# Slot starts of a mixture-of-experts layer: a running sum by doubling, replaced by a product with a triangle and one row sum

## The reference

```python
xn = _layernorm(x)
x = x + attention(xn, Wq, Wk, Wv, Wo) + moe(xn, gate_w, expert_w, expert_b)
# attention: 16 heads of 32, rotary positions, causal softmax
# moe, for each token:
gate_logits = xf @ gate_w.T                      # 8 experts
top_vals, top_idx = top_k(gate_logits, 2)
w = softmax(top_vals)                            # the two shares
y_all = einsum('td,eod->teo', xf, expert_w) + expert_b
out = sum(take_along_axis(y_all, top_idx) * w)
```

## Time and profile before

| what | value |
|---|---|
| median of 3 runs | 982.35 us (981.11 to 984.5) |
| the profiled execution's own time | 979.72 us |
| its span, first to last instruction | 977.9 us |
| PE busy | 915.0 us (94%) |
| DVE busy | 739.1 us (76%) |
| POOL busy | 559.2 us (57%) |
| ACT busy | 436.7 us (45%) |
| DMA queue of SP, share of 16 engines | 44.9% |
| mean granted TensorE clock | 0.992 |

### The profile page before, as it was taken

One profiled execution on the slowest core, in us unless ns is written; L12 is line 12 of the kernel. 1 busy time (PEld: TensorE's weight loads), 2 busy tenths in 40 slices (PEclk: granted clock), 3 DMA queues, 4 the chain that ended last, 5 costly groups with the idle time before them and its releaser, 6 DMA issues.

```text
span 977.9 us, 18755 instructions
## 1 busy us (share of the span) xinstructions
PE 915.0 (94%) x6589; PEld 450.1 (46%) x6589; DVE 739.1 (76%) x1327; ACT 436.7 (45%) x711; POOL 559.2 (57%) x553
## 2 busy tenths in 40 slices
PE   2899898989999989989999999998999999999887
PEld 1344344444444544545555555544444444444333
DVE  7988988898889899944444444467788888888865
ACT  5367877766765443421122211134344444344432
POOL 1545686674776446753333333148877888777741
PEclk9999999999999999999999999999999999999999
DMA  6365688688786362586655555455655564555431
GB/s 245 108 227 186 193 272 320 197 309 299 222 287 245 120 217 88 201 285 191 197 175 176 177 174 173 151 195 163 205 179 182 170 196 141 164 184 184 151 110 55
DMA packets 107963, 188.63 MB, mean 193 GB/s; under 512 B 11872, under 2 KB 65248, under 8 KB 102624
## 3 DMA queue, kind: packets, MB, share of 16 engines
q1 hardware_dynamic: 97072, 152.03, 44.9%
q0 software_dynamic: 10800, 35.40, 12.9%
HBM read 117.13 MB, written 70.25 MB: 192 GB/s over the span
## 4 chain that ended last, share of the span: by engine, by line
PE 69%; DVE 14%; ACT 6%; DMA 4%; issue 3%; POOL 3%; SPq 1%; DVEq 0%; ACTq 0%; POOLq 0%
PE psum L945 19%; PE psum L1030 11%; PE psum L1054 7%; PE psum L993 6%; PE psum L980 5%; PE psum L996 5%; PE psum L962 5%; PE psum L1039 4%; DVE top L1479 4%; PE psum L922 3%; ACT pT L760 2%; PE psum L964 2%; DMA sum_sb<-x 2%; ACT x_in L693 1%; DMA w_rows<-w_hl 1%
## 5 line engine op out<-in xcount | busy, mean ns | idle before, releaser
L760 ACT ACTIVATE pT<-psum,factors 128x512 f32<-128x512 f32 (+1 forms) x352 | 217.9, 642 | 239.9 <-PE psum L980 231.3
L1479 DVE TENSOR_REDUCE top<-psum 128x1 f32<-128x384 f32 (+3 forms) x352 | 209.9, 635 | 19.9 <-PE psum L964 18.9
L1030 PE MATMUL psum<-xT,w_att 128*128 128x512 f16 x768 | 196.6, 382 | 7.7 <-DVE xT L1430 5.1
L945 PE MATMUL psum<-w_exp,x_gT 128*128 x852 | 195.3, 379 | 0.8 <-DVE x_gT L1435 0.8
L610 POOL DMA_INDIRECT x_g<-xn_rows,tok_of x71 | 67.3, 948 | 131.8 <-PE psum L922 129.1
L962 PE MATMUL psum<-k_stack,q_stack 96*128 96x384 f16 (+3 forms) x512 | 127.4, 302 | 13.8 <-DVE top L1479 13.1
L980 PE MATMUL psum<-q_stack,k_stack 98*128 98x256 f16 (+3 forms) x512 | 128.6, 303 | 11.6 <-ACT pT L760 9.1
L1435 DVE TENSOR_TENSOR x_gT<-psum,x_gT 128x512 f16<-128x512 f32 x71 | 49.0, 691 | 104.1 <-ACT x_gT L784 86.8
L945 PEld LDWEIGHTS psum<-w_exp,x_gT 128*128 128x128 f16 x852 | 83.4, 98 | 85.8 <-issue 1.1
L784 ACT ACTIVATE x_gT<-psum 128x512 f16<-128x512 f32 x71 | 42.3, 597 | 170.2 <-PE psum L922 165.3
L600 POOL TENSOR_TENSOR o_hl<-o_sb,o_hl 128x512 f16<-128x512 f32 x31 | 36.5, 1177 | 124.3 <-ACT o_hl L774 122.5
(11 more groups left out here) (175 smaller groups left out, 1291.9 us busy)
## 6 DMA issues: line engine op xcount, KB each, us to landing
y_rows<-y_sb SPq DMA_DIRECT2D x71, 256.0 KB
w_in<-w_all SPq DMA_DIRECT2D x12, 1024.0 KB, 11.9
q_stack<-qk_rows SPq DMA_DIRECT2D x96, 128.0 KB
k_stack<-qk_rows SPq DMA_DIRECT2D x96, 128.0 KB
x_in<-x SPq DMA_DIRECT2D x8, 1024.0 KB, 10.1
qk_rows<-q_hl SPq DMA_DIRECT2D x32, 256.0 KB
qk_rows<-k_hl SPq DMA_DIRECT2D x32, 256.0 KB
xn_rows<-x_in SPq DMA_DIRECT2D x8, 1024.0 KB, 5.2
```

Source lines behind the costliest of these rows:

```text
L760: act.activation(p_of(j, h, heads), banks[BANK_T + (NT_ * n + k) % 2][:, 0:W], ACT.Exp, scale=factors[:, 0:1]).then_inc(exp_done, 1)
L945: now = pe.matmul(banks[s % 4], x_gT[s % 4][:, xp * C + c, :], w_exp[:, bass.ds(e, 1), wp, c, :].rearrange("p e d -> p (e d)"), start=n == ...
L1030: now = pe.matmul(bank, w_att[:, what, wp, c, g * P:(g + 1) * P], xT[b % 2][:, xp * C + c, :], start=at_pass == 0, stop=at_pass == 3 * C - 1)
L1479: return dve.tensor_reduce(out=top[:, h:h + heads, i], in_=banks[BANK_S + k % 2][:, 0:heads * W].rearrange("p (h t) -> p h t", h=heads), a ...
```

## The change

The running sum is made by one product of the 8 counts with a constant lower triangle (8 x 8 products per partition) and one sum over the last axis. `ends` is a single row of 8. The triangle comes behind the constants in `small`, so that its load grows from 384 to 448 numbers per partition; `small_sb` grows by 256 bytes per partition and `ends` shrinks by 32, so that all tiles laid out behind them stand 224 bytes further. The product goes to a new tile `tiles_to` in room that is free at that time. The three operations of `w12` are cut out of `experts_of_tiles` (end of step 14) into `shares_of_experts`, called behind `low_xg(2)`, ahead of the loop over the expert tiles.

```diff
--- before.py
+++ after.py
@@ -87,6 +87,7 @@
     small_sb = at("small_sb", [P, small.shape[1]], F32)
     prefer = small_sb[:, 0:NT * E].rearrange("p (t e) -> p t e", t=NT)
     tile_no = small_sb[:, NT * E:NT * E + NTILE]
+    up_to = small_sb[:, NT * E + P:NT * E + P + E * E].rearrange("p (e f) -> p e f", e=E)
     count16 = at("count16", [P, P], F16)
     token_i = at("token_i", [P, NT], I32)
     token16 = at("token16", [P, NT], F16)
@@ -119,7 +120,7 @@
     low16 = at("low16", [P, 2, NT], F16)
     cnt_i = at("cnt_i", [P, E], I32)
     tiles = at("tiles", [P, E], F32)
-    ends = at("ends", [P, 2, E], F32)
+    ends = at("ends", [P, E], F32)
     starts = at("starts", [P, E], F32)
     top = at("top", [P, HG, J], F32)
     c_scale = at("c_scale", [P, HG * J], F32)
@@ -182,6 +183,7 @@
     chosen = at("chosen", [P, NT, E], F16)
     place_f = at("place_f", [P, NT, E], F32)
     picked = at("picked", [P, 2, NT, E], F32)
+    tiles_to = at("tiles_to", [P, E, E], F32)
     assert place[0] <= slot[3]
     place[0] = slot[4]
     at_low = at("at_low", [P, 2, NT, P], F16)
@@ -1364,12 +1366,9 @@
             def place_slots():
                 dve.wait_ge(rank_read, 1)
                 own.link(dve.tensor_copy(tiles[:], cnt_i[:]))
-                own.link(dve.tensor_copy(ends[:, 0, :], tiles[:]))
-                for n in (1, 2, 4):
-                    a, z = (0, 1) if n != 2 else (1, 0)
-                    own.link(dve.tensor_copy(ends[:, z, 0:n], ends[:, a, 0:n]))
-                    own.link(dve.tensor_tensor(ends[:, z, n:E], ends[:, a, n:E], ends[:, a, 0:E - n], ALU.add))
-                own.link(dve.tensor_tensor(starts[:], ends[:, 1, :], tiles[:], ALU.subtract))
+                own.link(dve.tensor_tensor(tiles_to[:], up_to, tiles[:].unsqueeze(1).broadcast_to([P, E, E]), ALU.mult))
+                own.link(dve.tensor_reduce(out=ends[:], in_=tiles_to[:], axis=AX.X, op=ALU.add))
+                own.link(dve.tensor_tensor(starts[:], ends[:], tiles[:], ALU.subtract))
                 own.link(dve.tensor_scalar(starts[:], starts[:], float(P), None, ALU.mult))
                 own.link(dve.tensor_tensor(place_f[:], place_f[:], starts[:].unsqueeze(1).broadcast_to(all_tiles), ALU.add))
                 for k in range(2):
@@ -1384,10 +1383,12 @@
 
             def experts_of_tiles():
                 both = [P, NTILE, E]
-                own.link(dve.tensor_tensor(past[:], tile_no.unsqueeze(2).broadcast_to(both), ends[:, 1, :].unsqueeze(1).broadcast_to(both),
+                own.link(dve.tensor_tensor(past[:], tile_no.unsqueeze(2).broadcast_to(both), ends[:].unsqueeze(1).broadcast_to(both),
                                            ALU.is_ge))
                 own.link(dve.tensor_reduce(out=n_past[:], in_=past[:], axis=AX.X, op=ALU.add))
                 dve.tensor_scalar(exp_of[:], n_past[:], float(E - 1), None, ALU.min).then_inc(exp_of_done, 1)
+
+            def shares_of_experts():
                 dve.wait_ge(gap_exp, 1)
                 own.link(dve.tensor_scalar(w12[:, 0, :], w12[:, 1, :], 1.0, None, ALU.add))
                 own.link(dve.reciprocal(w12[:, 0, :], w12[:, 0, :]))
@@ -1667,6 +1668,7 @@
             low_xg(1)
             normalise_o(N1 - 1)
             low_xg(2)
+            shares_of_experts()
             for s in range(NTILE):
                 if s + 3 < NTILE:
                     low_xg(s + 3)
@@ -1713,7 +1715,7 @@
     sign = np.where(np.arange(HEAD) < HEAD // 2, -1.0, 1.0)[:, None]
     down = 2.0 ** -LOG_QK
     trig = np.stack([np.tile(np.cos(emb) * down, (4, 1)), np.tile(np.sin(emb) * sign * down, (4, 1))], axis=1).astype(np.float32)
-    small = np.concatenate([np.tile(E - np.arange(E), T // P), np.arange(P)]).astype(np.float32)
+    small = np.concatenate([np.tile(E - np.arange(E), T // P), np.arange(P), np.tril(np.ones((E, E))).ravel()]).astype(np.float32)
     arrays = {
         "x": x,
         "w_all": np.ascontiguousarray(np.stack(mats)),
```

## The result

The changed kernel took 986.95 us in the median of 13 runs (984.29 to 990.49), against 982.72 us for the kernel before in 13 runs (979.62 to 985.46): ratio 1.0048, 95% interval 1.0033 to 1.0063. It is slower by 0.5%, where a gain of 0.9 us was forecast. The profiled execution took 984.72 us.

The account below looks back on a forecast made before the run. PE was taken to bound the kernel (busy 915.0 of 977.9 us), DVE counting only where it holds PE up. Median 982.35 less 0.9 gives 981.4 us, no measurable change; range 979.2 to 984.6 us.

Parts of the forecast that it names:

- Part 1 and 2: DVE in `place_slots`: seven doubling operations (4.33 us) go, product and row sum (0.5 us) come; 3.8 us gained without POOL.
- Part 3: `place_slots`: POOL's unshortened operations delay the product, L1374 and the pair L1376; DVE gains only 0.9 us (0.4 to 1.7).
- What reaches PE: PE's 1.14 us wait for DVE's row maximum ahead of 354.50: PE gains 0.9 us (0.4 to 1.14).
- Part 4: Three share operations leave step 14's end, gaining nothing, for DVE's 2.34 us idle time ahead of `low_xg` at 435.16, costing nothing.
- Part 5: Larger load of `small` at the start and tiles behind `ends` standing 224 bytes further: price zero.
- the blocks only move: Rival in `place_slots`: POOL wins each race; DVE gains 0.4 us, PE 0.4 or nothing; 982.0 to 982.35 us; chance 0.23.
- The knot of step 15: Rival: the small product delayed at 415.35 and PE's wait for it open, up to 4.5 us gained, 976.9 us; chance 0.09.
- The one slower rival: POOL passes DVE's small product in step 13 or 14, PE idles and its clock falls; 985.9 us; chance 0.07.

Follow-up runs that it names:

- the gap alone: The kernel before with 224 unused bytes behind `ends` and nothing else changed: 987.9 us, ratio 1.0047 to the kernel before.
- the control on the boundary: The kernel before with 256 unused bytes behind `ends`, so large tiles move but still start at multiples of 256 bytes: 984.53 us, ratio 1.0006.
- the padded kernel: The changed kernel with 32 unused bytes behind `ends`, large tiles again at multiples of 256 bytes: 981.73 us, ratio 0.9984 to the kernel before.

## Why the prediction was wrong, point by point

**Part 1 and 2 (the doubling, the sum): right.** The row sum took the 0.22 us it was given. The product waited for POOL, as the copy did, and took 1.27.

**Part 3 (POOL's say moves on): right in the mechanism.** The product was to end with L586, the first 256-element addition to take over 1 us, the pair to stand beside the masks; all three are in the rows above. The alternation was priced at 2 x 0.36 us for the pair: it took 1.51 - 0.88 = 0.63 more than alone, and DVE gained 1.15 us, not 0.9 (bounds 0.4 and 1.7).

**What reaches PE: right, a fifth low.** PE's wait went from 1.14 to nothing, where 0.2 to 0.3 was to be left; the wait of 1.27 behind it stayed at 1.28. In the table of distances this is the step of 1.14 us between 302 and 355, and it is the whole of the wait: more DVE time than that could not have been used there.

**Part 4 (the shares): right.** Idle time ahead of L1439's counterpart 1.49 us in the kernel after, forecast about 1.5; the three operations stand from 435.22 to 436.00 there, and with them moved back the time is the same. They lie in the idle time that was named for them, which comes later than 432 to 435 because the whole kernel is 2.7 us late there. For the same reason the expert stage begins later than before, not 0.9 us sooner.

**Part 5 (the rest): here it failed.** The sentence was that tiles behind `ends` stand 224 bytes further, that no row shows what an address costs, and that it is therefore zero. The price was 4.5 us, 1.0047 by the gap alone. Two errors lie in it. A missing row was taken as a price of zero, where it should have been bounded from both sides: SP's queue is busy for 44.9% of 16 engines, 439 us, and 1% more of that is not nothing in a kernel whose DMA share is 0.80 from 100 to 300 us. What the runs show in place of the zero is packets that take 343 us more in all (21 us for each of 16 engines) and a kernel that is 4.5 us longer. And the cover named for it, that weights and stacks are loaded steps ahead, holds for loads only. Stores weren't weighed, and they can have no such lead: in the trace of before ACT waits twice for the store of an expert's weights, 2.5 us in all, and PE stands behind ACT (the rows of step 6 above). That the loss comes by this wait is not shown: the control on the boundary has the longer one.

**The rivals.** That the blocks only move: no, DVE gained 1.15. The knot of step 15 neither opened nor moved: c_f took 2.66 us there against 2.64, and PE idled 2.76 us ahead of L971, against 2.74. The one slower rival gave 985.9 us for a knot tied elsewhere; the measured time is near it by chance: the mechanism is not the one, and the kernel with the gap alone excludes it.

**The range** left the case out for that reason: its upper end, 984.6, held nothing for the addresses; only a chance of 0.01 was put on them and other unknowns as a loss.

**What stays open.** That moving the large tiles by 224 bytes costs the time, and that packets then take longer, is shown; the path from the packets to PE is not. The places of the loss can't be told from one trace of each kernel, since single executions differ by as much. Single tiles were not moved alone, and how much is waiting for stores and how much is loads was not separated. Whether the boundary is one of 256 or of 128 bytes is left open by the times.

## What to carry to other kernels

A change of a small tile's size moves every tile behind it. Add up the offsets before and after; if large tiles leave a 256-byte boundary, as here, time a version with the small tile padded (here 32 bytes were worth 4.8 us, about four times the 1.1 us that the profiles give the edit itself). When the time moves and the edited place doesn't show it, line up the two traces instruction by instruction. But line up a control as well, here the padded kernel: what grows in its trace too is the difference between executions, and a wait that it shares proves no cause.

## What was not expected of the hardware

The distance from the boundary does not act evenly: 128 bytes off cost 0.05% (-0.14% to 0.24%), 32 bytes 0.35%, 64 bytes 0.30% and 224 bytes 0.47%, and the mean time of a 512-byte packet follows it, 42.2, 48.6, 46.5 and 50.2 ns against 37.0. The intervals of 128 and 32 bytes still overlap a little (to 0.24% and from 0.19%). Larger packets feel it less: those of 1024 bytes took 55.2 ns in the mean after the change and 51.8 before, those of 8192 bytes 340.1 and 339.2.
